# A fused Mamba, mixture-of-experts, attention and gated-cell kernel: an order with TensorE's attention output product ahead of the next sequence's value products

## What is computed

```
xn = layernorm(x)
x1 = x + ssm(xn) + moe(xn)          # layer 0
xn = layernorm(x1)
out = x1 + attn(xn) + cell(xn)      # layer 1

ssm:  xi, z = split(xn @ W_in);  delta, B, C from xi @ W_xp;  a = exp(-exp(A_log) * softplus(delta))
      h_t = a_t * h_{t-1} + B_t * xi_t;  y = (C * h + D * xi) * silu(z);  y @ W_out
moe:  top-1 of 8 experts, each layernorm scale/bias -> 32 hidden -> gelu -> 128
attn: 16 heads; scores = Q K^T;  Wmat = scores * decay (exp of running sums of gates)
      * lam (one weight per level of a binary tree over the tokens);  layernorm(Wmat V @ Wout + x)
cell: over the 16 sequences in turn: f, i, g gates from x_t and c;  c = f*c + i*g;
      tanh(x_t @ wo + c_final @ uo + bo)
```

## Time and profile before

| | |
|---|---|
| median of 3 runs | 963.75 us (962.29 to 964.87) |
| the profiled execution: its own time | 963.9 us |
| its span in the profile | 962.1 us |
| mean granted TensorE clock | 0.99 |
| busy: PE, VectorE, ScalarE, POOL | 96%, 87%, 73%, 26% |
| chain that ended last, by engine | PE 61%, VectorE 22%, issue 6%, ScalarE 5%, POOL 3% |

### The profile page before, as it was taken

One profiled execution on the slowest core, in us unless ns is written; L12 is line 12 of the kernel. 1 busy time (PEld: TensorE's weight loads), 2 busy tenths in 40 slices (PEclk: granted clock), 3 DMA queues, 4 the chain that ended last, 5 costly groups with the idle time before them and its releaser, 6 DMA issues.

```text
span 962.1 us, 27082 instructions
## 1 busy us (share of the span) xinstructions
PE 925.1 (96%) x9981; PEld 680.8 (71%) x9981; DVE 833.9 (87%) x2112; ACT 699.1 (73%) x1575; POOL 254.7 (26%) x321
## 2 busy tenths in 40 slices
PE   6889999999999999999999999999999999999994
PEld 3675867778687776867677686877768676776862
DVE  5888798988979899897989979798897989889787
ACT  4676795959769595876949678594967859497684
POOL 1025031230313122131321223132032312303368
PEclk9979999999999999999999999999999999999998
DMA  4000000000010000101000010000001000000627
GB/s 168 12 11 2 24 1 24 11 11 22 0 33 0 22 11 0 33 0 33 0 22 11 0 33 0 29 4 22 11 0 33 0 22 11 11 21 0 207 79 219
DMA packets 31913, 27.70 MB, mean 29 GB/s; under 512 B 1552, under 2 KB 25744, under 8 KB 31760
## 3 DMA queue, kind: packets, MB, share of 16 engines
q1 hardware_dynamic: 31888, 27.37, 8.8%
HBM read 15.57 MB, written 11.80 MB: 28 GB/s over the span
## 4 chain that ended last, share of the span: by engine, by line
PE 61%; DVE 22%; issue 6%; ACT 5%; POOL 3%; DMA 1%; DVEq 0%; ACTq 0%; SPq 0%; POOLq 0%
PE p L729 6%; PE p L715 6%; PE p L782 5%; PE p L764 4%; DVE pair L1746 4%; PE p L746 3%; DVE pair L1760 3%; PE p L524 3%; PE p L688 3%; PE p L760 2%; PE p L525 2%; PE p L526 2%; ACT vdw L1136 2%; PE p L583 2%; DVE xn L1516 2%
## 5 line engine op out<-in xcount | busy, mean ns | idle before, releaser
L1145 ACT ACTIVATE gx<-p 128x512 f32<-128x512 f32 x256 | 146.4, 602 | 3.9 <-PE p L652 2.1
L650 PE MATMUL p<-x1Th,Gl 128*128 128x512 f32 x256 | 107.1, 418 | 0.0
L651 PE MATMUL p<-x1Tl,Gh 128*128 128x512 f32 x256 | 101.1, 395 | 0.0
L652 PE MATMUL p<-x1Th,Gh 128*128 128x512 f32 x256 | 101.1, 395 | 0.0
L2035 POOL TENSOR_TENSOR vp<-vdw,e 128x256 f32<-128x256 f32 (+3 forms) x80 | 55.1, 722 | 165.6 <-DVE ms L1711 165.6
L1187 ACT ACTIVATE yu<-p,head_part 128x128 f32<-128x128 f32 x64 | 23.5, 367 | 100.0 <-PE p L782 99.9
L782 PEld LDWEIGHTS p<-pair,vbd 64*32 64x32 f32 x4096 | 44.6, 105 | 43.6 <-issue 43.5
L715 PEld LDWEIGHTS p<-rs,GT 128*128 128x128 f32 x512 | 60.7, 191 | 15.6 <-ACT ms L1233 13.4
L729 PE MATMUL p<-gx,x1T 128*32 128x512 f32 x512 | 68.2, 604 | 2.5 <-DVE pair L1766 1.7
L1233 ACT ACTIVATE ms<-p 128x120 f32<-128x120 f32 x256 | 48.3, 279 | 23.9 <-PE p L715 21.0
L2105 POOL TENSOR_TENSOR skip<-skip,W 128x512 f32<-128x512 f32 x15 | 19.1, 1275 | 172.6 <-DVE skip L1516 172.6
(11 more groups left out here) (348 smaller groups left out, 2785.9 us busy)
## 6 DMA issues: line engine op xcount, KB each, us to landing
xin<-in_x SPq DMA_DIRECT2D x16, 256.0 KB, 2.7
hx_scratch<-vdw SPq DMA_DIRECT2D x15, 256.0 KB, 2.5
res_scratch<-normed SPq DMA_DIRECT2D x14, 256.0 KB, 2.0
gx<-in_weights SPq DMA_DIRECT2D x1, 1216.0 KB, 9.6
vp<-hx_scratch SPq DMA_DIRECT2D x4, 256.0 KB, 3.5
GT<-res_scratch SPq DMA_DIRECT2D x4, 256.0 KB, 3.5
out<-vp SPq DMA_DIRECT2D x4, 256.0 KB, 3.2
W<-in_weights SPq DMA_DIRECT2D x1, 746.0 KB, 10.7
```

What stands on the lines that cost most here:

```text
L650: pe.matmul(head_bank(h)[:, :], tile(Gl, h), x1Th[:, :], start=True, stop=False)
L651: pe.matmul(head_bank(h)[:, :], tile(Gh, h), x1Tl[:, :], start=False, stop=False)
L652: pe.matmul(head_bank(h)[:, :], tile(Gh, h), x1Th[:, :], start=False, stop=True).then_inc(R["gx_ps"], 1)
L1145: act.activation(tile(gx, h, T), head_bank(h)[:, :], ACT.Copy).then_inc(R["gx_copied"], 1)
```

## The change

Nothing is computed differently. Calls stand elsewhere, and two waits are altered:

1. TensorE, end of a pass: `project_out(i)` before `values(j)` instead of after.
2. TensorE, `scan_b`: the product that waits for `xi0_ready` first, the one that waits for `delta_ready` second.
3. TensorE: `scan_c(j, 1)` right behind `scan_c(j, 0)`, ahead of `pair_scores(i, 0)`, instead of behind `pair_levels(i, 0)`. For it VectorE does `scan_inputs(j)` before `node_rows(i)`.
4. TensorE: head 4 before `turn_xn`, so that the two transposes follow each other. ScalarE copies head 4 before the two transposes' results.
5. POOL, first pass only: it waits for `g_ready` 1 (VectorE line 1666) instead of the second `xh`, splits `Mdelta` alone, then the inputs, then `Win` and `MBC`. `deltas` and `split_inputs` wait for 2 splits instead of 6.
6. SyncE: output 14 is stored after both halves of output 15 instead of before them.

```diff
@@ last() of SyncE
-                for b in (13, 14):
-                    sp.wait_ge(R["end_pool_add"], END_POOL.index(b) + 1)
-                    store(b, whole, end_hx[b])
+                sp.wait_ge(R["end_pool_add"], END_POOL.index(13) + 1)
+                store(13, whole, end_hx[13])
                 for half in range(2):
                     sp.wait_ge(R["end_add"], len(END_DVE) + 1 + half)
                     store(B - 1, slice(2 * half, 2 * half + 2), end_hx[B - 1])
+                sp.wait_ge(R["end_pool_add"], END_POOL.index(14) + 1)
+                store(14, whole, end_hx[14])
@@ deltas of TensorE
-                pe.wait_ge(R["wsplit_steps"], 6)
+                pe.wait_ge(R["wsplit_steps"], 2)
@@ scan_b of TensorE
+                project(j, 1, "xi0_ready", j + 1, bc_part(1), "b1_ps")
                 project(j, 0, "delta_ready", j + 1, bc_part(0), "b0_ps")
-                project(j, 1, "xi0_ready", j + 1, bc_part(1), "b1_ps")
@@ stages of TensorE
-                    heads(i, 0, 4)
+                    heads(i, 0, 5)
                 if j is not None:
                     turn_xn(j)
-                if i is not None:
-                    heads(i, 4, 5)
-                if j is not None:
                     turn_xh(j)
...
                 if j is not None:
                     scan_c(j, 0)
+                    scan_c(j, 1)
                 if i is not None:
                     pair_scores(i, 0)
                     left_halves(i)
                     pair_levels(i, 0)
-                if j is not None:
-                    scan_c(j, 1)
-                if i is not None:
                     node_matrices(i)
...
+                if i is not None:
+                    project_out(i)
                 if j is not None:
                     values(j)
-                if i is not None:
-                    project_out(i)
@@ stages of ScalarE
+                if i is not None:
+                    heads(i, 4, 5)
                 if j is not None:
                     turned_n(j)
-                if i is not None:
-                    heads(i, 4, 5)
-                if j is not None:
                     turned_h(j)
@@ stages of VectorE
                     node_lams(i)
+                if j is not None:
+                    scan_inputs(j)
+                if i is not None:
                     node_rows(i)
                 if j is not None:
-                    scan_inputs(j)
                     scans(j)
@@ POOL
+            def split_step_weights():
+
+                pool.wait_ge(R["z1_ps"], 1)
+                pool.wait_ge(R["g_ready"], 1)
+                split_weights(((Mdh, Mdl, Mdelta[:, :]),), 0)
+
             def split_scan_weights():
 
-                pool.wait_ge(R["z1_ps"], 1)
-                pool.wait_ge(R["xh_ready"], 2)
-                split_weights(((Mdh, Mdl, Mdelta[:, :]), (Winh, Winl, w("Win")), (MBCh, MBCl, MBC[:, :])), 0)
+                split_weights(((Winh, Winl, w("Win")), (MBCh, MBCl, MBC[:, :])), 2)
...
                 if not later(i):
+                    split_step_weights()
+                split_inputs(j)
+                if not later(i):
                     split_scan_weights()
-                split_inputs(j)
```

More of the change, by code:

```diff
@@ L1268, in stages @@
                     heads(i, 2, 4)
-                if j is not None:
-                    turned_n(j)
                 if i is not None:
@@ L1273, in stages @@
                 if j is not None:
+                    turned_n(j)
                     turned_h(j)
@@ L2047, in split_inputs @@
                 pool.tensor_tensor(xnTl[:, 0:1], xnT[:, 0:1], xnT[:, 0:1], ALU.subtract)
-                pool.wait_ge(R["wsplit_steps"], 6)
+                pool.wait_ge(R["wsplit_steps"], 2)
                 pool.tensor_copy(xnTh[:, :], xnT[:, :]).then_inc(R["xsplit_ready"], 1)
```

## The result

| | before | changed |
|---|---|---|
| median of 6 runs each, same chip | 964.54 us (962.29 to 965.63) | 968.44 us (967.93 to 969.4) |
| ratio, 95% interval | | 1.004 [1.0029, 1.0051] |
| the profiled execution: its own time, its span | 963.9, 962.1 us | 969.4, 967.6 us |
| granted TensorE clock | 0.99 | 0.99 |
| a pass of the loop | 56.73 us | 57.10 us |

The change makes the kernel slower by 0.4%.

The account below looks back on a forecast made before the run. It took TensorE as the bound for some 40 us of a pass, with VectorE's chain to `delta` bounding the rest. Loop, first pass, last pass and stores: 963.9 + 5.2 - 0.5 + 0.5 - 0.3 = 968.8 us, range 961 to 973.

Parts of the forecast that it names:

- Copies to `vdw` 0.55 late: End of a pass: the output product ahead delays the values, so ScalarE's copies start 0.55 us late, bounds 0 and 0.81.
- The swap in `scan_b` uses up the delay: At `delta`: with the other product (0.69 us) in front, head 14 starts within 0.05 us of where it did.
- Scores 0.8 late: Behind both `scan_c` halves: TensorE waits 0.25 us for VectorE's `xi` product, scores start 0.8 us late.
- `left_halves` takes back 0.1: Between scores and `pair_levels` part 0: small waits for POOL shrink by 0.1 us, leaving part 0 0.68 us late.
- Part 1 leaves 0.37 late: `pair_levels` part 1: TensorE waits 0.4 us for VectorE's second `pair_lams`; each pass 0.37 us longer, +5.2 us over 14.
- Faster rival: Loop: copies to `vdw` don't move, so a pass gains 0.17 us (-2.4 us in all); 958.7 us, chance 0.15.
- No change: Loop: a delay of 0.3 us, a pass gains or loses under 0.1 us; 963.5 us, chance 0.21.
- slower still: Loop or first pass: all 0.81 us passes (+9 us), or the first pass loses its clock; 973 us, chance 0.10.
- Transposes side by side: nothing: TensorE's two transposes: one fp32r/float32 change saved, 0.1 us, where TensorE waits anyway, so no gain.
- POOL in the first pass, -0.5: First pass: later weight splits shorten VectorE's gates but meet its differences; -0.5 us, bounds -3.3 and +1.5.
- Last pass +0.5: Last pass: late copies ahead of the gates, POOL's queue of sums the bound from `node_lams` on; +0.5 us.
- stores -0.3: End of the kernel: whole output 14 stored last, earlier but twice as large; -0.3 us, bounds -0.8 and +0.5.

Follow-up runs that it names:

- e1: The kernel before with one edit, the output product ahead of the value products: 970.99 us, ratio 1.0061.
- e2: The changed kernel with the output product back behind the value products, all other edits kept: 963.58 us, ratio 0.9983.
- e5: e2 with VectorE doing the second `pair_lams` before the first `pair_weights` instead of after: 957.23 us, ratio 0.9917.
- e3: The changed kernel with half of the output product (4 of 8 instructions) ahead of the value products, half behind: 962.82 us, ratio 0.9982.
- e4: The changed kernel with head 4 back between the two transposes, on TensorE and ScalarE: 968.96 us, ratio 1.0041.
- e9: The changed kernel with part 5 undone, POOL splitting all three weights before the first inputs: 969.92 us, ratio 1.0054.
- e10: The kernel before with part 5, POOL's changed first pass, alone: 964.01 us, ratio 0.9997.
- e6: The changed kernel with VectorE doing the second `pair_lams` before the first `pair_weights`: 962.66 us, ratio 0.997.
- e11: e5 with half of the output product (4 of 8 instructions) ahead of the value products: 957.11 us, ratio 0.9918.
- e7: The kernel before with VectorE doing the second `pair_lams` before the first `pair_weights`: 965.11 us, ratio 0.9995.

## Why the prediction was right, step by step

The forecast was 968.8 us and a pass of 57.1; measured were 968.44 and 57.10. The mechanism holds: e1 and e2 show that the output product ahead of the values is the whole loss, and e5 that the wait ahead of part 1 is VectorE's. Below the level of the sum, several terms were off, and some cancel. In the pass, the late copies were put at 0.55 us and the gain behind them at 0.17; they are 0.41 and 0.03. Both are 0.14 too large, and the difference comes out right by luck. In the whole, my change of +4.9 us was 1.0 more than the +3.9 measured, and the base of 963.9 us was 0.6 below the median of 964.54; that the two times are only 0.4 apart is luck too.

- *Copies to `vdw` 0.55 late*: 0.41. Line 615 moves by 3.25 - 2.53 = 0.72 and not by the 0.81 of the earlier trace rows, and a copy starts 0.34 behind the start of its product, not 0.44. The 0.12 from the earlier trace rows came from another kind of product. The lower bound of 0 was that of a delay within the slack, which e3 shows for half the product.
- *The swap in `scan_b` uses up the delay*: right, head 14 starts at 21.29 on the ruler, against 21.32. In e2, where the copies are on time, it starts at 20.88: the swap and the edits that go with it would gain 0.44. But the way by which the delay travels was only half of what I wrote. The chain of the changed kernel:

```profile
512.15 0.55 ACT vdw L1132
...
513.83 1.05 ACT gx L1141 x2
514.92 0.50 PE p L651
```

  Between the two rows of ScalarE are the small steps of the norm. From 514.92 on it stays on TensorE, past `delta`. VectorE's work up to `delta` is as late as the copies (19.48 against 19.08), but it is no longer what holds TensorE: the heads' copies, which queue behind the copies to `vdw` on ScalarE, hold head 4, which waits for the copy of head 1 (0.35 us), and TensorE has no gap afterwards up to part 0. I had put these waits of the heads inside the time in which TensorE waits for VectorE anyway; in fact TensorE leaves head 4 at 514.92 - 507.31 = 7.61 on the ruler, against 512.13 - 504.93 = 7.20, and keeps the 0.41. With head 4 behind the first transpose (e4) its wait is gone, TensorE starts the second transpose right behind VectorE's norm instead (515.92, the norm's end at 515.77), and the pass is the same. That is where VectorE's 14 points of the chain went. A delay of the copies has two ways to TensorE, and the swap closed one.
- *Scores 0.8 late*: 0.76. The cause that I gave, a wait of 0.25 us for VectorE's product with `xi`, is hardly there: line 1584 comes at 22.67, and the half product starts 530.71 - 530.45 = 0.26 us behind the product ahead of it, where 0.23 is the rule among its neighbours. It is the 0.7 us of the second half of `scan_c` and its start. *`left_halves` takes back 0.1*: 0.19 (4.19 us from scores to part 0, then 4.00). Part 0 is thus 0.57 late and not 0.68.
- *Part 1 leaves 0.37 late*: 0.37, and this is luck to 0.1 us. I had 3.35 us from part 0 to part 1 (1.27 to the first `pair_lams`, 2.08 to the end of the second). It is 3.49: the two pieces were right (538.28 + 0.68 - 535.62 = 3.34), and I left out 0.14 us, the time from the end of VectorE's operation at 538.96 to the start of TensorE's at 539.10. That made up for the 0.11 too much in part 0.
- *Faster rival, -0.17 per pass with the copies in place*: 0.03 in e2, for the missing 0.14. What it was said to lack, 0.2 us of slack, was counted to the start of line 615 and not to its result: the product comes 0.72 us later into a slack of 0.32, 0.40 too much. And its 958.7 us was never to be had from this change; e2, which is that rival, takes 963.58. What gives those 0.46 us per pass is the order of three VectorE operations (e5).
- *No change, slower still*: neither. The first took a delay of 0.3, the second all of the 0.81; 0.41 passed.
- *Transposes side by side: nothing*: e4 agrees within its interval.
- *POOL in the first pass, -0.5*: open. The runs give -1.4 (e9) and -0.3 (e10), each with an interval that takes in nothing and the -0.5. Its pieces are clearer: the gates took 0.23 us each as said, the copy to `cgt` comes 3.35 us earlier behind the first of them where I had 3.3, and the differences took 4.39 in place of 2.50. By the rule of the Trainium skill (SBUF — State Buffer, "Who interferes with whom") I had estimated some 2.3 us for that collision; the trace shows 1.89, with POOL's own two operations 0.46 and 0.33 longer, which fits a lock that holds up both sides. I was too careful about the clock: in the changed kernel it did not fall behind the second stall.
- *Last pass +0.5, stores -0.3*: the stretch from the last copies to `vdw` to the end is 56.95 against 56.85 us. The two together are 0.1, about their sum of 0.2. Neither was tried alone, so their sizes stay open. The end of SyncE's queue answers to the earlier trace rows; the two halves of output 15 (`held`) come first now, and the whole output 14 (`W`) is last:

```profile
962.59 1.43 SPq L347 DMA_DIRECT2D out<-held  x2
964.05 0.51 SPq L347 DMA_DIRECT2D out<-W  x1
```

  From the end of the last issue to the end of the span are 967.60 - 964.56 = 3.04 us, against 962.10 - 959.42 = 2.68 before, 0.36 more with the larger transfer last.

From the medians, 3.9 us of loss is 5.1 in the loop less 1.3 outside it. My sum had 5.2 in the loop less 0.3 (-0.5 + 0.5 - 0.3) = 4.9, so what stands outside the loop is the term that was off. Taking the 14 passes from the total of each kernel in the same way leaves -1.0 to -1.8 us in all eight kernels that have parts 5 and 6 of the change together, -0.2 in e9 (all but part 5) and -0.2 in e10 (part 5 alone), with intervals of 0.8 to 1.4 us either way. So there is a gain outside the loop, but which of the parts brings it stays open.

## What to carry to other kernels

Before work is put ahead of a producer, measure that producer's slack: here a table load on ScalarE covered 0.32 us, half the moved product fitted and cost nothing, and the whole product cost its excess of 0.4 us in each of the 14 passes. When a wait is taken away and the time stays, look at the very next wait in the same pass and at what stands ahead of its releaser: one small operation that nobody waits for stood between two that somebody does, and exchanging them turned 0.03 us per pass into 0.49. And price an operation's hand-over to the next engine (0.05 to 0.14 us here) like the operation; over 14 passes it was 2 us, most of what one rival rested on.

## What the runs showed that I had not expected

- The chain's shares moved from VectorE (22% to 8%) to TensorE (61% to 79%) in a kernel that is slower, and in e2, which is a little faster, they are the same (78% and 8%). They tell which of two nearly equal paths comes last, and not how much stands to be gained.
- A granted clock of 1.2 GHz behind an idle time is not certain. It fell behind TensorE's waits of 2.43 us and 2.32 us (e9), and not behind 2.83 us (e10):

```profile
68.95 0.50 PE L524 MATMUL p<-xnTh,MBCl 128*128 128x512 f32 x1 [2.83 <-DVE decay L1580]
```

  The same wait in the same place, 2.13 us in the changed kernel and 2.14 in e6 and e11, leaves 2.4 GHz in the first and 1.2 GHz in the other two; e6:

```profile
70.00:72.00 2.00, 2.00 (x6) 1.52 (x6) 2.00 (x4) 1.35 (x3) 0.00 (x0) 0.50 0.00 0
```

- The first pass varies by more than its part of the change. From the first copies to `vdw` to the second it took 66.3, 66.3, 68.2 and 68.2 us in the kernels with POOL early (before, e7, e1, e9) and 64.6 to 66.2 in the nine others. I had expected 66.3 for e9. The 1.9 us by which e1 and e9 are longer go with one more stretch at 1.2 GHz, behind a wait of 1.96 us near 90 us; e9:

```profile
90.00:94.00 4.00, 4.00 (x81) 2.60 (x77) 3.71 (x9) 0.37 (x1) 0.00 (x0) 0.59 0.02 4
```

  The changed kernel waits 1.95 us there and keeps 1.00 from 90 to 94 us. So e9's profiled execution makes part 5 look worth more than it is, and terms of 1 us in this pass can only be told over several runs.
